# A conditioning recurrence and a routed feed-forward network: a re-ordered front, idle products, bounds shared by VectorE, a first transposition in halves

## The reference

```python
x = x + ffn(cond(x, cond_1024, Wx, Wh, b), shared_w1, shared_w2, experts_w1, experts_w2, gate_w)   # x: 2 x 1024 x 256

def cond(x, h0, Wx, Wh, b):                       # a recurrence over 1024 steps
    xp = einsum('ntd,dh->nth', x, Wx) + b
    h_t = tanh(xp_t + h_{t-1} @ Wh)

def ffn(x, ...):                                  # 2048 tokens, hidden 1024, 8 experts, the best 2
    shared = silu(x @ shared_w1.T) @ shared_w2.T
    gates = softmax over the two largest of x @ gate_w.T, zero elsewhere
    selected = sum over e of gates[:, e] * (silu(x @ experts_w1[e].T) @ experts_w2[e].T)
    return shared + selected
```

## Time and profile before

| what | us |
|---|---|
| median of 3 runs | 385.19 (381.85 to 387.07) |
| the profiled execution | 381.38 |
| its span | 379.7 |
| PE busy in it | 356.2 (94%) |
| ACT busy | 244.1 (64%) |
| DVE busy | 200.2 (53%) |
| POOL busy | 108.5 (29%) |
| mean granted TensorE clock | 0.991 |

### The profile page before, as it was taken

One profiled execution on the slowest core, in us unless ns is written; L12 is line 12 of the kernel. 1 busy time (PEld: TensorE's weight loads), 2 busy tenths in 40 slices (PEclk: granted clock), 3 DMA queues, 4 the chain that ended last, 5 costly groups with the idle time before them and its releaser, 6 DMA issues.

```text
span 379.7 us, 8904 instructions
## 1 busy us (share of the span) xinstructions
PE 356.2 (94%) x2458; PEld 253.0 (67%) x2459; DVE 200.2 (53%) x415; ACT 244.1 (64%) x478; POOL 108.5 (29%) x99
## 2 busy tenths in 40 slices
PE   5989999997997998999999999999999999999981
PEld 4758889964664675666667666667766666666660
DVE  0089999979996988964333323333323333232310
ACT  3777788888556778865555665556665556665530
POOL 1100010000276788600123333223333133332241
PEclk9999999999999999999999999999999999999996
DMA  6999999607697979999898998889988989989992
GB/s 194 422 421 434 428 407 334 194 4 124 87 199 182 225 180 226 235 194 196 176 129 153 168 155 155 147 149 156 158 149 154 148 142 158 148 159 147 152 127 28
DMA packets 158173, 73.50 MB, mean 194 GB/s; under 512 B 140736, under 2 KB 155200, under 8 KB 156992
## 3 DMA queue, kind: packets, MB, share of 16 engines
q1 hardware_dynamic: 146672, 59.83, 66.9%
q0 software_dynamic: 6864, 9.11, 16.9%
q10 hardware_dynamic: 4608, 4.20, 4.1%
HBM read 23.68 MB, written 16.53 MB: 106 GB/s over the span
## 4 chain that ended last, share of the span: by engine, by line
PE 80%; ACT 6%; DMA 5%; issue 3%; DVE 2%; another core or an unknown queue 1%; ACTq 1%; POOL 0%; SPq 0%; DVEq 0%; POOLq 0%
PE py L1138 32%; PE z L1033 30%; PE z L1047 8%; PE z L982 3%; PE z L1014 3%; DMA space<-recurrence_w 2%; DMA space<-space 2%; ACT space L799 1%; ACT space L876 1%; PE px L1025 1%; PE py L982 1%; PE z L995 1%; DMA space<-x_cols 1%; ACTq L896 1%
## 5 line engine op out<-in xcount | busy, mean ns | idle before, releaser
L1138 PE MATMUL py<-w_slots,space 128*128 (+1 forms) x1272 | 148.4, 273 | 7.4 <-DMA space<-recurrence_w 3.7
L1033 PE MATMUL z<-w_slots,x 128*128 (+1 forms) x636 | 145.9, 379 | 0.8 <-issue 0.8
L1138 PEld LDWEIGHTS py<-w_slots,space 128*128 128x128 f16 x1272 | 123.8, 98 | 33.1 <-issue 3.5
L1033 PEld LDWEIGHTS z<-w_slots,x 128*128 128x128 f16 x636 | 62.1, 98 | 65.0 <-issue 1.2
L453 POOL DMA_INDIRECT out<-space x37 | 57.5, 1553 | 157.0 <-issue 65.2
L876 ACT ACTIVATE space<-z,tile_scales 128x512 f32<-128x512 f32 x106 | 71.8, 678 | 41.3 <-PE z L1033 34.1
L582 DVE SCALAR_TENSOR_TENSOR recurrence_w<-space,tile_scales,recurrence_w 128x512 f16<-128x512 f32 x54 | 40.5, 750 | 71.7 <-ACT recurrence_w L881 65.6
L582 DVE SCALAR_TENSOR_TENSOR space<-space,tile_scales 128x512 f16<-128x512 f32 x52 | 39.0, 750 | 57.7 <-ACT space L881 42.4
L528 DVE SCALAR_TENSOR_TENSOR w_slots<-w_slots,w_scale 128x1024 f16<-128x1024 f32 x36 | 46.2, 1283 | 1.3 <-issue 0.3
L881 ACT ACTIVATE recurrence_w<-space,tile_scales 128x512 f16<-128x512 f32 x54 | 39.0, 722 | 8.7 <-ACT space L876 2.5
L430 POOL DMA_INDIRECT sorted_rows<-space x32 | 39.1, 1221 | 17.5 <-issue 13.1
(11 more groups left out here) (114 smaller groups left out, 178.9 us busy)
## 6 DMA issues: line engine op xcount, KB each, us to landing
w_slots<-weights SPq DMA_DIRECT2D x9, 2048.0 KB, 30.5
sorted_rows<-pad_row SPq DMA_DIRECT2D x1, 5070.0 KB, 60.2
space<-x_rows ACTq DMA_DIRECT2D x16, 128.0 KB
out<-space ACTq DMA_DIRECT2D x16, 128.0 KB
space<-x_cols SPq DMA_DIRECT2D x1, 1024.0 KB, 8.6
space<-recurrence_w SPq DMA_TRANSPOSE x54
space<-space SPq DMA_TRANSPOSE x52
x<-sorted_rows SPq DMA_TRANSPOSE x39
```

The lines of the kernel that those rows point to most:

```text
L1033: last = nc.tensor.matmul(Z[u % 2][h][:], x16[:, u, x_part, k], weight(f, k * HID + h * BANK, BANK, part), start=k == 0 and x_part == 0 an ...
L1138: last = nc.tensor.matmul(PY[p][:, 0:D], hiddenT[:, p, low, q], weight(f, MATRIX + q * D, D, part), start=q == 0 and not low and part == 0 ...
```

## The change

The front: `wx` and the first block of x are still the first two loads of SP. The bias and the start state h0 go to ACT's own DMA queue, ahead of ACT's first activation. SP's order behind x block 0 becomes gate, wh, x block 1, x blocks 2 and 3, the first half of network 0's weights, x blocks 4 and 5, their second half, x blocks 6 and 7, networks 1 to 8. POOL fills `ones` first, and PE multiplies `ones` by itself seven times (WARM_UP) ahead of its wait for `wx`. PE projects blocks 0 and 1 ahead of the guess, and then issues `guess_step(i, u)` ahead of `project(i + 2, u)`; ACT issues the tanh of a step ahead of `project_out`. The last tanh of a pass is written straight to the starts of the next, and `next_start` of ACT, with its semaphore `start_ok`, goes.

The bounds: DVE finds network 0 in two halves and shares its bound between the partitions by itself (`share_bound`: reductions, two transpositions of 32 x 32 squares, and copies between quarters of the partitions); POOL's first batch goes. Then comes one `split`, then 6 of network 1's 8 chunks, so that 14 chunks are found by DVE instead of 16. ACT's finds have no loop any more (steps written out), and five pairs instead of four are left at the end: one after the recurrence, four in tiles 1 to 4. `find_scales` of the last batch and `route_scales` are both in g = 5. The late splits are spread by a table. POOL's last `reduce_bounds` therefore waits for ACT's find in g = 4.

The first transposition: the high part of tile 0 is turned in two DMAs of half the width, the first as soon as ACT has written the first half. `down(0)` waits for the halves separately. PE loads the drift count ahead of the last half of `up` of tile 1, where it did so behind it.

```diff
-ARRIVALS = ((0, 1), (1, 2), (2, 4), (4, BLOCKS))
+ARRIVALS = ((0, 1), (1, 2), (2, 4), (4, 6), (6, BLOCKS))
-EARLY_WIDES = 6 * WIDES - 2
+EARLY_WIDES = 22
-BOUND_BATCHES = ((0, 2), (2, 3), (3, 4), (4, 5), (5, 6), (6, FFNS))
-FOUND_BY_DVE = BOUND_BATCHES[0][1]
-WIDE_FINDS_FROM = FOUND_BY_DVE + L // CHUNKS
+BOUND_BATCHES = ((0, 1), (1, 2), (2, 3), (3, 4), (4, 5), (5, 6), (6, FFNS))
+FOUND_BY_DVE = 2 * CHUNKS - 2
+WIDE_FINDS_FROM = FOUND_BY_DVE + L
+LATE_FINDS_FROM = WIDE_FINDS_FROM + 2 * L
+LATE_FINDS = (FFNS * CHUNKS - LATE_FINDS_FROM) // 2
+SPLITS_AT = {3: (22, 23), 5: (24,), 6: (25, 26), 7: (27,), 8: (28, 29), 9: (30,), 10: (31,), 11: (32, 33), 12: (34,), 13: (35,)}
+HIGHS_FROM = 6
...
+            sp.dma_start(wx_sb, wx).then_inc(wx_in, 16)
+            load_x(0)
             sp.dma_start(gate_sb[:], gate_cols).then_inc(gate_in, 16)
+            sp.dma_start(wh_sb, wh).then_inc(wh_in, 16)
+            load_x(1)
+            load_x(2)
+            load_weights(0, 0, CHUNKS // 2, w_up_in)
+            load_x(3)
+            load_weights(0, CHUNKS // 2, CHUNKS, w_in[0])
+            load_x(4)
+            for f in range(1, FFNS):
+                load_weights(f, 0, CHUNKS, w_in[f])
...
+            def turn_first():
+                sp.wait_ge(h_hi_ok, 1)
+                sp.dma_start_transpose(hiddenT[:, 0, 0, 0:TPB], hidden_rows[0][:, 0, 0:BANK]).then_inc(first_turned, 16)
...
-            for n in range(len(BOUND_BATCHES) - 1):
+            for n in range(1, len(BOUND_BATCHES)):
                 reduce_bounds(n)
-            reduce_bounds(len(BOUND_BATCHES) - 1)
             pool.wait_ge(routed, 1)
...
+            def share_bound():
+                link(nc.vector.tensor_reduce(peaks[:, 0:2], chunk_bound[:, 0].rearrange("p (m s) -> p m s", m=2), AX.X, ALU.max))
+                link(nc.vector.transpose(peaks_turned, peaks))
+                link(nc.vector.tensor_reduce(peaks[:, 2:3], peaks_turned, AX.X, ALU.max))
+                for b in range(P // SQUARE):
+                    last = nc.vector.tensor_copy(quarters[0:SQUARE, b:b + 1], peaks[b * SQUARE:(b + 1) * SQUARE, 2:3])
+                link(last)
+                link(nc.vector.tensor_reduce(quarters[0:SQUARE, 4:5], quarters[0:SQUARE, 0:4], AX.X, ALU.max))
+                link(nc.vector.tensor_copy(peaks[0:SQUARE], quarters[0:SQUARE, 4:5].broadcast_to([SQUARE, SQUARE])))
+                link(nc.vector.transpose(peaks_turned[0:SQUARE], peaks[0:SQUARE]))
+                for b in range(P // SQUARE):
+                    last = nc.vector.tensor_copy(bound[b * SQUARE:(b + 1) * SQUARE, 0], peaks_turned[0:SQUARE, 0:2])
+                link(last)
...
-            for f in range(FOUND_BY_DVE):
-                last = find_largest(f)
-            last.then_inc(bound_ok, 1)
+            link(nc.vector.memset(peaks, 0.0))
+            find_largest(0, 0, CHUNKS // 2, w_up_in)
+            link(find_largest(0, CHUNKS // 2, CHUNKS, w_in[0]))
             find_scales(0)
...
-            split_upto(FOUND_BY_DVE * WIDES)
+            split_upto(1)
+            find_largest(1, 0, FOUND_BY_DVE - CHUNKS, w_in[1]).then_inc(bound_ok, 1)
+            split_upto(WIDES)
...
+            nc.scalar.dma_start(states[:, :, 0, 0:B], h0_cols).then_inc(h0_in, 16)
+            nc.scalar.dma_start(bias_sb[:], bias).then_inc(bias_in, 16)
             act.wait_ge(guess_ok, 1)
...
+            pe.wait_ge(consts, 1)
+            for _ in range(WARM_UP):
+                nc.tensor.matmul(PX1[:, 0:P], ones[:], ones[:], start=True, stop=True)
             pe.wait_ge(wx_in, 16)
...
-            for m in range(K):
-                project(0, m)
+            for n in range(2 * K):
+                project(n // K, n % K)
             pe.wait_ge(guess_ok, 3)
             for i in range(BLOCKS):
                 for u in range(2):
-                    if i + 1 < BLOCKS:
-                        project(i + 1, u)
                     guess_step(i, u)
+                    if i + 2 < BLOCKS:
+                        project(i + 2, u)
...
-            for h in range(HALVES):
-                up_half(1, SHARED, h, up_mm)
+            up_half(1, SHARED, 0, up_mm)
             pe.wait_ge(drift_known, 1)
             same = pe.value_load(same_count_u[0:1, 0:1], min_val=0, max_val=EXPECTED_SAME)
+            up_half(1, SHARED, 1, up_mm)
```

More of the change, by code:

```diff
@@ L288, in weight @@
             return w_split[:, bass.ds(f * (2 * WCOLS) + (2 * c + part) * WIDE + start, n)]
-        highs_by_act = [late[0] for late in LATE_SPLITS]
+        highs_by_act = [late[0] for g, late in SPLITS_AT.items() if g >= HIGHS_FROM]
         def wide(c):
@@ L410, in reduce_bounds @@
                 start, end = BOUND_BATCHES[n]
-                if n == 0:
+                if n == 1:
                     pool.wait_ge(bound_ok, 2)
-                else:
-                    pool.wait_ge(found, found_upto(end))
+                pool.wait_ge(found, found_upto(end))
                 nc.gpsimd.partition_all_reduce(chunk_bound_all[:, start:end].rearrange("p f c -> p (f c)"),
@@ L501, in find_scales @@
             def find_scales(n):
                 start, end = BOUND_BATCHES[n]
-                dve.wait_ge(bound_all_ok, n + 1)
                 flat = lambda v: v[:, start:end].rearrange("p f m -> p (f m)")
-                link(nc.vector.tensor_reduce(flat(bound), chunk_bound_all[:, start:end].rearrange(
-                    "p f (m s) -> p (f m) s", m=2), AX.X, ALU.max))
+                if n == 0:
+                    share_bound()
+                else:
+                    dve.wait_ge(bound_all_ok, n)
+                    link(nc.vector.tensor_reduce(flat(bound), chunk_bound_all[:, start:end].rearrange(
+                        "p f (m s) -> p (f m) s", m=2), AX.X, ALU.max))
@@ L778, in _, with next_start @@
             act.wait_ge(bias_in, 16)
+            def next_start(m):
+                return states[:, m, 0, B:COLS]
             def project_out(i, m):
@@ L784, in project_out @@
                                      bias=bias_sb[:, m:m + 1]).then_inc(xproj_ok, 1)
-            for m in range(K):
-                project_out(0, m)
+            for n in range(K + 1):
+                project_out(n // K, n % K)
             for i in range(BLOCKS):
                 for u in range(2):
-                    if i + 1 < BLOCKS:
-                        project_out(i + 1, u)
                     for m in range(K):
                         act.wait_ge(z_mm[m], i * 2 + (u + 1))
-                        nc.scalar.activation(guess[:, 1 - u, m], ahead[i % 3][m][:, u * COLS:(u + 1) * COLS], ACT.Tanh,
-                                             bias=bias_sb[:, m:m + 1]).then_inc(h_ok[m], 1)
+                        if i * 2 + u + 1 == L:
+                            nc.scalar.activation(next_start(m), ahead[i % 3][m][:, u * COLS:(u + 1) * COLS - B], ACT.Tanh,
+                                                 bias=bias_sb[:, m:m + 1]).then_inc(h_ok[m], 1)
+                        else:
+                            nc.scalar.activation(guess[:, 1 - u, m], ahead[i % 3][m][:, u * COLS:(u + 1) * COLS], ACT.Tanh,
+                                                 bias=bias_sb[:, m:m + 1]).then_inc(h_ok[m], 1)
+                    n = i * K + u + K + 1
+                    if n < BLOCKS * K:
+                        project_out(n // K, n % K)
@@ L802, in find_last @@
             def find_last(c):
-                find_bound(LAST * CHUNKS + 2 * c, 2)
-            def next_start(r, ends):
-                for k in range(K):
-                    act.wait_ge(h_ok[k], r * L)
-                act.sem_inc(act_waited, 1)
-                nc.scalar.copy(states[:, :, 0, B:COLS], ends[:, :, 0:COLS - B]).then_inc(start_ok, 1)
+                act.wait_ge(found, 2 * L + c)
+                find_bound(LATE_FINDS_FROM + 2 * c, 2)
             def step_pair(z, h, r, i, p, find_at=None, chunks=1, starts_next=False):
@@ L848, in _ @@
             step_pair(z_mm, h_ok, r, L // 2 - 1, 1, find_at, chunks)
-            act.wait_ge(w_in[LAST], 16)
-            for c in range(WIDES // 2):
-                act.wait_ge(found, found_upto(LAST) + c)
-                find_last(c)
+            find_last(0)
             act.wait_ge(drift_known, 1)
@@ L1134, in down @@
                         prefix_sums()
-                    pe.wait_ge(turned[low][p], n)
+                    halved = isinstance(g, int) and g == 0 and not low
+                    pe.wait_ge(first_turned if halved else turned[low][p], n)
                     for q in range(Q):
+                        if halved and q == TPB:
+                            pe.wait_ge(turned[0][0], n)
                         for part in range(1 if low else 2):
```

111 lines of the change are left out of this document (51 added, 60 removed).

## The result

| | before | changed |
|---|---|---|
| median of 20 runs each, one chip | 382.92 us (381.44 to 387.95) | 385.78 us (381.49 to 390.89) |
| ratio | | 1.0057 [1.0034, 1.0080] |
| profiled execution, its span | 381.38, 379.7 | 383.26, 381.5 |
| mean granted TensorE clock | 0.991 | 0.981 |

The ratio compares undisturbed executions, so it isn't the quotient of the medians. The forecast was 3.2 us faster; the kernel became 0.6% slower. The time itself lies in the range of the forecast, its direction doesn't.

A forecast was written before the change was run, and what follows sets the result against it. Bound: PE's sorted stream, reached behind two chains ending within 1 us of each other (recurrence on PE and ACT, splits on DVE). Terms -0.8 - 0.8 - 0.9 - 1.4 + 0.7 = -3.2 us gave 382.0 us, range 377.5 to 386.5.

The forecast's parts named there:

- (a): Front: idle products and the new guess order bring the guess's last step sooner; -0.8 us, ends -1.9 and +0.9.
- rival 1: Front: loads are late, partly from small packets, so it isn't shorter; (a) becomes +0.9, time 383.7 us; chance 0.17.
- (b): Recurrence: both ACT copies, ahead of rounds 1 and 2, go; -0.8 us, from -1.1 to -0.6.
- (c): Round 1: ACT has no loop, so eight steps get shorter; -0.8 to -0.9 us, ends 0 and -1.5.
- (d): DVE's chain of finds, sharing and early splits: ends at 77.5, 2.3 us sooner, agreeing with (c) to 0.2.
- (e): Recurrence to tiles: fewer waits through the earlier drift-count load and halved transposition; -1.4 us, ends -2.2 and 0.
- (f): Tiles 1 to 5: DVE has a scale chain, route_scales and a whole split in g = 5; +0.7 us, 0 to 2.1.
- (g): POOL's sorting, beside the tiles, starts later; costed at 0, its risk left to rival 2.
- rival 2: POOL's sorting becomes the bound and PE's sorted tiles wait; 387.7 us if nothing is absorbed; chance 0.12.
- Rival 3: Tiles: ACT's 4.98 us stall ahead of 116.26 goes, another 3.2 us sooner, 378.8 us; chance 0.16.

The follow-up runs named there:

- e11: e10 with one whole first transposition and PE's drift-count load behind both halves of up(1); 1.0025 of before, against 0.9934 for e10.
- e12: Changed kernel with the split of tile 5 moved to tile 6 and two later splits moved by one tile; 1.0142 of before.
- the early bounds: POOL's last reduce_bounds moved from ahead of all sorting rows to between rows 1 and 2, in the changed kernel; 0.9920 of before on chip 9, 0.9934 on chip 8.
- e16: Changed kernel with POOL issuing a sorting row's transfers only when those of two rows before have landed, on chip 8; 0.9959 of before.
- e17: Changed kernel with the early bounds, gate's load behind x, and at most two sorting rows in flight, on chip 1; 0.9869 of before.
- e10: Changed kernel with POOL's last reduce_bounds moved between sorting rows 1 and 2, on chip 8; 0.9934 of before.
- e9: The changed kernel, unaltered, measured again on chip 8; 1.0017 of before.
- e4: Changed kernel with SP's loads reordered: x block 1, wh, x blocks 2 and 3, then gate; on chip 9, 0.9993 of before.
- e13: The kernel before, unaltered, profiled on chip 8; 1.0013 of before.
- e18: The kernel before, with POOL limited to two sorting rows in flight, on chip 1; 0.9990 of before.

## Why the prediction was wrong, point by point

- (a), -0.8: the last step of the guess came at 26.71, 0.5 us sooner. The idle products ran from 1.06 as said, but the first eight products took 2.31 us, the next eight 1.99, and x block 1 was 1.07 us late, of rival 1's kind. Both vary from one execution to the next by more than the term. The idle products themselves are not shown to gain anything beyond that.
- (b), -0.8, and (c), -0.9: the two transitions shrank by 0.6 (27.70 - 26.71 against 1.57) and 0.4 us, and round 1 by another 0.7 (22.18 from its start to round 2's, before 23.29, less the 0.4). Right in mechanism and within 0.2 us in size.
- (d): the last early split ended at 77.17 (said 77.5). `share_bound` took 2.6 us, from 18.01 to 20.64, against 2.2.
- (e), -1.4: mis-sized, it gave nothing against before. (By its own numbers it should have read -1.6: of 2.2 us of waiting 0.6 would be left where 1.40 stood.) From the first `up` to the fourth it is 14.17 us, before 14.10. The idle time ahead of `up(2)` stayed (0.98), and the second half of the transposed high part landed 5.5 us after its issue at 84.51, so PE waited 1.63 between the halves. The whole one of e11, issued at 85.24, was there at 90.35, no slower. e11 shows that the edit is still worth having: without it the kernel is slower by 0.9%.
- (f), +0.7: no run isolates it; e12, which takes the split out of tile 5, brought no gain.
- **(g), "costed at 0", is the step that failed.** The text asked only whether the last sorted row would be late for SP's load, and gave 2.2 us of spare. All it said of POOL's times came about (first transfer 108.81, last end 160.2), and rival 2's wait was not seen in the profile of the changed kernel. What the runs showed in its place is a cost of 0.5 to 0.8% of the kernel (1.7 to 3.2 us), the difference that the early bounds make on chips 7, 9 and 8. A sort that starts later starts with a backlog: before, POOL had two rows ready at about 103.4, issued eight transfers without a pause and then waited for row 4 until 117.94; now it had four rows ready at 108.81, got two more in time, and issued twelve. On the chips that have ACT's idle time, a longer idle time goes with it, and a shorter one with the limit of e16 and e17. Giving the 8 us back (e10 against e9) brings 3.2 us, the whole size of the forecast; but ACT's idle times in e10 add up to 10.76 us, no less than e9's 10.29, so it isn't by their sum that e10 gains. On chips 9 and 7, where no idle time is, e4 shows PE waiting 0.79 us for the late rows: once the stream comes sooner, the 2.2 us of spare are gone. In the first profile the stream was itself 3.1 us late at the first sorted `up` (174.08 against 170.96), which hid that wait.
- Rival 3 named the idle time of ACT and priced only its going. Its growing was the right rival: 6.9 us at `up(8)` in the profiled execution, part of which is the clock at 0.51.

Shown: that the late start of the sort took most of the gain, since the early bounds alone return the forecast's ratio on two chips. Argued, from one profile a kernel: that POOL's transfers in flight lengthen the idle time, since it is 2.89 and 2.19 us in the two changed kernels with the limit and 5.6 to 11 us in those without. Open: by what POOL's transfers in flight hold ACT and PE, why only on some chips, and what the shorter idle times (2 to 6 us, in e10, e13, e16, e17, e18) are. e10 has 5.61 us with an early sort, so the backlog isn't their only cause.

## What to carry to other kernels

When a step of a transfer-issuing engine is moved later, ask not only when its last transfer is needed but also how many it will then issue back to back, and what was idle beside them before. An unexplained idle time in the profile is a term with two signs: price its growing as well as its going. And measure a change of under 1% on more than one chip: here the same edit was 1.1% slower on one and, if anything, faster on another.

## What was not expected of the hardware

- Chips differ in more than speed: an idle time of ACT of 2 to 11 us ahead of a copy whose input is ready is in all 12 profiles from elsewhere than chips 9 and 7, and in none of the 8 of these two. In the long ones PE's matmuls come singly beside it.
- A releaser in the profile is an inference: in e16 the idle time of 2.89 us looks like a wait for PE, and only the count of the rows shows that the product named is that of the next row.
- Behind 3 us in which PE was busy for 0.83, its granted clock fell from 1.00 to 0.51 and stayed there for most of 10 us.
- The row of the granted clock shows 1.00 in the first 9.5 us in every kernel, also where the matmuls run at half pace; there the mean ns of a group is the measure, not the clock's row.
- A copy of one or two columns between quarters of the partitions on DVE is about 0.16 us each (four in 0.61 us, and four of two columns in 0.68).
